# Statistics products behind the row transform, 2 KB pieces of mode weights, and whole 128-column products in a two-part convolution kernel

## The chip, the cores and the metric

The kernel runs on one core of one Trainium2 chip. The metric is the device time of one execution in microseconds (us). A core has TensorE (PE, matrix products into PSUM), VectorE (DVE), ScalarE (ACT), GpSimd (POOL) and SyncE (SP), which here issues the DMA transfers. The engines run their own instruction streams and wait for each other by semaphores.

## The reference

x is 8 images of 32 channels of 64x64, all float32. Group norm with 32 groups normalizes each channel of each image. Two residual parts follow each other:

```python
def _L0_conv_ref(x, weight, fc_w, fc_b):
    x_ft = jnp.fft.rfftn(x, axes=(-2, -1))
    blk = jnp.einsum('bimn,hiomn->bhomn', x_ft[:, :, :m1, :m2], w_c)
    ...
    xr = jnp.fft.irfftn(out_ft, s=(H, W), axes=(-2, -1))
    return jnp.einsum('bchw,oc->bohw', xr, fc_w) + fc_b[None, :, None, None]

def _L1_conv_ref(x, dft_weight, ksm_w, bias, fbm_scale):
    att = jax.nn.softmax(jax.nn.sigmoid(x.mean(axis=(2, 3)) @ ksm_w.T), axis=1)
    agg = jnp.einsum('bk,koihwc->boihwc', att, dft_weight)
    kernels = jnp.clip(jnp.fft.ifft2(cw, axes=(-2, -1), norm='ortho').real, -10.0, 10.0)
    ...
    return (out + bias[None, :, None, None]) * fbm_scale

x = x + _L0_conv_ref(_gn(x), L0_conv_weight, L0_conv_fc_w, L0_conv_fc_b)
x = x + _L1_conv_ref(_gn(x), L1_conv_dft_weight, L1_conv_ksm_w, L1_conv_bias, L1_conv_fbm_scale)
```

## The kernel before, in words

The order of work is written out by hand for each engine. The first part works on 32 by 32 modes of each channel; the second has one 3x3 convolution per image. A float32 product is two records of the trace, and each has a weight load (LDWEIGHTS, PEld) and a pass (MATMUL, PE). A product can use all 128 columns of the array, or 64 or 32 of them; products on different column parts run side by side. Each stage of the first part is a Fourier transform along one axis, written as products with constant matrices.

1. **Row transform**, `f1(k)` (L797, products on L807), eight pieces: 32 products of 64 columns by 64 each, all into PSUM slot 2, half a piece in each bank. ACT copies the first half out (`copy_y`, L420), DVE the second (L545). ACT squares x (L431), DVE sums the squares (L552).
2. **Statistics**, `sums(s)` (L811), after two pieces each: a product for the means (L817) and one for the squares (L819), both with a 128-column stationary matrix. DVE reads them in `pick(s)` (L557 to L562). After the fourth, variance, square root and reciprocal (L577, L578, L440, L580) give the factor 1/std that every operand needs.
3. **Column transform**, `f2` (L822 to L849): for each k of 0 to 3 and xx of 0, 1 a PSUM bank, filled for 8 images by two 64-column products each, 32 products per k. `pair(k, s)` makes two images of both banks of k.
4. **Operands**, `operand(n)` with n = 2k + xx (L583): DVE writes the normalized bank to `zn` (L591), which has two buffers, and the block of group 0 (32 partitions) straight to `bd[k]` (L594). ACT copies groups 1 to 3 from `zn` to `bd[k]` (L449). The two buffers make DVE wait for ACT's `bd_act`. POOL clears x_buf, the home of bd[2] and bd[3] (L357, L359), after operand 0.
5. **Modes**, `mix(ml)` (L851): 64 products of 32 columns with the mode weights in w_buf. It waits for operands 2ml and 2ml+1, for its weights, and for its slot: mix(3) takes slot 0, which DVE must first have emptied of mix(0) (`mixed_dve` 2, L621). DVE's copies out of the mix stand behind all operands and behind three small steps on constants (L610, L614, L615). ACT makes the copy (3,0) on L456.
6. `fc` (L867), waiting for all mix copies and for `fcd_ready` (L610), then the inverse transforms `i1` and `i2`, and then the attention kernels and the convolution `conv` (L953), with the rest of the time. The diff doesn't touch them.

SP issues, in this order: the rows of x, the four mode weights of 1 MB (L305), late constants, the kernel weights `dft_w` (1152 KB, L308), params; and then, after `mix_done` 6 and 8, x once more (L318).

The functions that the diff touches:

Of the kernel before, what the change touches and what calls it, by code (L numbers as in the profile page):

```python
# [102 lines left out]
def spectral_then_attention_conv(nc, x, w_modes, dft_w, params, consts, out):  # L103
    with ExitStack() as ctx:
# [34 lines left out]
        def const(name):  # L139
# [17 lines left out]
              for t in (bd_buf[:], r_buf[:], x_buf[:, 0:4096], x_buf[:, 4096:8192])]  # L157
        zn = [t_buf[:, at:at + 512].rearrange("p (n b r) -> p n b r", n=M1, b=B) for at in (2304, 2816)]
        ost = bd_buf[:, 0:2048].rearrange("p (s n) -> p s n", s=2)

        def x_part(k):
# [103 lines left out]
        def mixed_part(ml, xx):  # L265

            ps = slot[slot_of["mix", ml]][:, 512 * xx:512 * xx + 512]
            return mixed[:, :, :, 4 * xx + ml, :], ps.rearrange("p (nl b g) -> p nl b g", nl=8, b=B)
# [28 lines left out]
        def _(sp):  # L297
# [6 lines left out]
            for ml in range(4):  # L304
                sp.dma_start(modes[:, ml].rearrange("p n xo -> p (n xo)"), w_modes[:, ml]).then_inc(modes_in[ml], 16)  # L305
                if ml == 1:
                    sp.dma_start(cst[:, LATE:NCONST], consts[:, LATE:NCONST]).then_inc(cst_in, 16)
# [109 lines left out]
        def _(act):  # L417
# [23 lines left out]
            def blocks(n):  # L441

                k, xx = divmod(n, 2)
                act.wait_ge(zn_ready, n + 1)
                if k >= 2:
                    act.wait_ge(bd_zero, k + 1)
                for g in range(1, 4):
                    ps = slice(32 * g, 32 * g + 32)
                    ins = act.activation(bd[k][ps, g, xx], zn[n % 2][ps], ACT.Copy)  # L449
                ins.then_inc(bd_act, 1)  # L450
# [82 lines left out]
        def _(v):  # L533
# [9 lines left out]
            def copy_y(k):  # L543
                v.wait_ge(f1_done, 2 * k + 2)
                nc.vector.tensor_copy(*y_part(k, 1)).then_inc(y_dve, 1)  # L545
# [19 lines left out]
            for k in range(7):  # L565
                sum_squares(k)
                copy_y(k)
                if k == 2:
                    v.wait_ge(fwd_w_in, 16)
                if k in (3, 5, 6):  # L570
                    pick(k // 2 - 1 if k < 6 else 2)
            sum_squares(7, 0)
            sum_squares(7, 1)
            copy_y(7)
            pick(3)

# [6 lines left out]
            def operand(n):  # L583

                k, xx = divmod(n, 2)
                z = f2_bank(k, xx).rearrange("p (b r n) -> p n b r", r=2, b=B)
                rstd = rstd1.unsqueeze(1).unsqueeze(3).broadcast_to([128, M1, B, 2])
                v.wait_ge(f2_done, n + 1)
                if n >= 2:
                    v.wait_ge(bd_act, n - 1)  # L590
                nc.vector.tensor_tensor(zn[n % 2], z, rstd, ALU.mult).then_inc(zn_ready, 1)  # L591
                if k >= 2:
                    v.wait_ge(bd_zero, k + 1)
                ins = nc.vector.tensor_tensor(bd[k][0:32, 0, xx], z[0:32], rstd[0:32], ALU.mult)  # L594
                if n == 0:
                    chain(ins)
                    chain(nc.vector.scalar_tensor_tensor(out=dc1, in0=mean1, scalar=float(NPIX), in1=rstd1,
                                                         op0=ALU.mult, op1=ALU.mult))

                    dc = bd[0][0:32, 0, 0, 0, :, 0]  # L600
                    ins = nc.vector.tensor_tensor(dc, dc, dc1[0:32], ALU.subtract)  # L601
                ins.then_inc(bd_ready, 1)

            v.wait_ge(bd_zero, 2)
            for n in range(8):
                operand(n)

            v.wait_ge(cst_in, 16)
            v.wait_ge(prm_in, 16)
# [6 lines left out]

            for ml in range(4):
                for xx in range(2):
                    if (ml, xx) != (3, 0):
                        v.wait_ge(mix_done, 2 * ml + xx + 1)  # L620
                        nc.vector.tensor_copy(*mixed_part(ml, xx)).then_inc(mixed_dve, 1)  # L621
            for k in range(4):
# [173 lines left out]
        def _(pe):  # L796
# [25 lines left out]
            def f2_part(k, xx, s):  # L822

                ps = f2_bank(k, xx)
                ml = 4 * xx + k
                for b in (2 * s, 2 * s + 1):
                    col = 64 * b
                    for h in range(2):
                        f = 4 * ml + 2 * h
                        last = pe.matmul(ps[64 * h:64 * h + 64, col:col + 64],  # L830
                                         y_rows[:, b, f:f + 2, :].rearrange("w g c -> w (g c)"), const("fwd_w")[:, 0:64],
                                         start=True, stop=True)
                if s == 3:
                    last.then_inc(f2_done, 1)
# [133 lines left out]
            f1(5)  # L968
            f1(6)
            sums(2)  # L970
            pair(0, 2)
            f1(7)
            for s in range(3):
                pair(1, s)
            sums(3)
            pair(0, 3)
            pair(1, 3)
            f2(2)
            f2(3)
            for ml in range(4):  # L980
                mix(ml)
# [78 lines left out]
```

## Time and profile before

| | us |
|---|---|
| median of 3 runs | 147.77 |
| lowest, highest | 147.33, 148.44 |
| the profiled execution, whole | 147.89 |
| its span in the trace | 146.1 |

| engine | busy us | share of the span |
|---|---|---|
| PE | 125.8 | 86% |
| PEld | 91.6 | 63% |
| DVE | 78.3 | 54% |
| ACT | 68.2 | 47% |
| POOL | 44.5 | 30% |

The shares are means over stages with different limits, so each stage has to be read by itself: the chain of work that ended last says what released each step, the timeline of an engine says when its groups began, how long they took together and what ended the idle time before them, and a table of windows gives the granted TensorE clock (PEclk) of a stretch, 1.00 for 2.4 GHz and 0.50 for 1.2 GHz. "issue" is time in which an engine waited for nothing that the profile shows. Of the DMA queues, q1 carries the kernel's transfers and q8 carries blocks of instructions.

### The profile page before, as it was taken

To read this page: it belongs to the slowest core of one execution; us is meant where nothing else is said; L and a number is where in the kernel's file an instruction comes from. 1 tells how busy PE (TensorE), PEld (TensorE's weight loads), DVE (VectorE), ACT (ScalarE), POOL (GpSimd) and SP (SyncE) were. 2 spreads that over 40 slices of the span, in tenths; PEclk is the share of its full clock that TensorE was granted. 3 is DMA by queue.
4 is the path that set the end of the run, shared out by engine and by line. 5 is a ranking of instruction groups with operands and counts; after the bars stand their busy time and mean duration, and the time that the engine had idled before them with its cause. 6 is when DMAs were issued, how large, how long until landed. Compare 5 with 4: busy or idle time off the path is not lost.

```text
span 146.1 us, 4992 instructions
## 1 busy us (share of the span) xinstructions
PE 125.8 (86%) x2172; PEld 91.6 (63%) x2172; DVE 78.3 (54%) x194; ACT 68.2 (47%) x134; POOL 44.5 (30%) x40
## 2 busy tenths in 40 slices
PE   0899999594996479899999979997999999999970
PEld 0889998594986369799999968932234322333310
DVE  0089679358758944633378468995751842201220
ACT  0575754519999415513347751499720560111010
POOL 7980000007999999999300000000000000000000
PEclk9999999999599869999999999999999999999999
DMA  4999989996000388868705977295898106563384
GB/s 97 273 265 238 242 216 408 416 416 246 5 0 9 78 179 186 194 152 191 174 12 114 173 141 155 62 176 80 174 170 185 24 18 145 129 144 71 89 177 99
DMA packets 68837, 23.09 MB, mean 158 GB/s; under 512 B 67408, under 2 KB 67664, under 8 KB 68304
## 3 DMA queue, kind: packets, MB, share of 16 engines
q1 hardware_dynamic: 68816, 22.78, 64.7%
q8 instruction: 17, 0.28, 0.8%
q14 instruction: 4, 0.03, 0.1%
HBM read 14.38 MB, written 4.19 MB: 127 GB/s over the span
## 4 chain that ended last, share of the span: by engine, by line
PE 62%; ACT 13%; DVE 12%; issue 7%; DMA 2%; SPq 1%; ACTq 0%; DVEq 0%
PE slot L953 21%; PE slot L807 10%; PE slot L883 10%; PE slot L896 7%; PE slot L872 4%; ACT bd_buf L449 3%; PE slot L830 2%; DMA x_buf<-x 2%; PE slot L863 2%; ACT r_buf L449 2%; ACT conv_w L499 2%; ACT q_buf L476 2%; ACT x_buf L449 2%; DVE y_buf L641 2%; DVE conv_w L728 2%
## 5 line engine op out<-in xcount | busy, mean ns | idle before, releaser
L953 PE MATMUL slot<-w_buf,conv_w 128*32 128x512 f32 x192 | 42.3, 593 | 0.0
L953 PE MATMUL slot<-y_buf,conv_w 128*32 128x512 f32 x192 | 42.2, 593 | 0.0
L953 PEld LDWEIGHTS slot<-w_buf,conv_w 128*32 128x32 f32 x192 | 12.1, 109 | 22.1 <-issue 21.9
L807 PE MATMUL slot<-cst,x_buf 128*64 128x64 f32 x512 | 18.8, 238 | 4.8 <-DMA x_buf<-x 4.2
L807 PEld LDWEIGHTS slot<-cst,x_buf 128*64 128x64 f32 x512 | 18.1, 152 | 5.0 <-issue 5.0
L752 DVE TENSOR_SCALAR bd_buf<-slot,st 128x512 f32<-128x512 f32 x8 | 6.0, 748 | 19.9 <-PE slot L953 19.9
L896 PE MATMUL slot<-cst,t_buf 128*128 128x128 f32 x128 | 15.5, 278 | 0.8 <-issue 0.8
L896 PEld LDWEIGHTS slot<-cst,t_buf 128*128 128x128 f32 x128 | 14.7, 192 | 1.4 <-issue 1.2
L883 PE MATMUL slot<-cst,r_buf 128*64 128x128 f32 x256 | 14.6, 274 | 0.7 <-ACT r_buf L461 0.7
L883 PEld LDWEIGHTS slot<-cst,r_buf 128*64 128x64 f32 x256 | 13.9, 137 | 1.0 <-ACT r_buf L461 0.9
L552 DVE TENSOR_REDUCE row_sq<-q_buf 128x16 f32<-128x1024 f32 (+1 forms) x9 | 9.8, 1098 | 7.8 <-ACT q_buf L431 7.7
L476 ACT ACTIVATE q_buf<-y_buf 128x512 f32<-128x512 f32 x16 | 9.9, 622 | 7.8 <-DVE y_buf L641 7.8
L508 ACT ACTIVATE bd_buf<-slot,st 128x512 f32<-128x512 f32 x8 | 5.3, 681 | 17.5 <-PE slot L953 12.4
L641 DVE SCALAR_TENSOR_TENSOR y_buf<-slot,stat,x_buf 128x512 f32<-128x512 f32 x16 | 11.2, 747 | 2.4 <-PE slot L896 2.4
L953 PEld LDWEIGHTS slot<-y_buf,conv_w 128*32 128x32 f32 x192 | 10.6, 109 | 2.6 <-issue 2.6
L499 ACT ACTIVATE conv_w<-kern 32x96 f32<-32x96 f32 x24 | 6.7, 280 | 9.8 <-DVE kern L723 9.2
L357 POOL MEMSET x_buf<- 128x4096 f32 x1 | 3.5, 3517 | 23.2 <-DVE bd_buf L601 23.2
L631 DVE COPY t_buf<-slot 128x512 f32<-128x512 f32 x8 | 5.5, 692 | 8.2 <-PE slot L883 8.2
L863 PE MATMUL slot<-x_buf,w_buf 128*32 128x64 f32 x256 | 5.7, 258 | 3.6 <-DVE q_buf L621 2.1
L467 ACT ACTIVATE t_buf<-slot 128x512 f32<-128x512 f32 x8 | 4.8, 595 | 8.2 <-PE slot L883 8.2
L431 ACT ACTIVATE q_buf<-x_buf 128x1024 f32<-128x1024 f32 (+1 forms) x9 | 8.5, 954 | 0.0
L830 PE MATMUL slot<-cst,y_buf 128*64 128x64 f32 x192 | 7.0, 224 | 1.5 <-issue 1.5
(115 smaller groups left out, 188.5 us busy)
## 6 DMA issues: line engine op xcount, KB each, us to landing
x_buf<-x SPq DMA_DIRECT2D x16, 256.0 KB, 4.1
w_buf<-w_modes SPq DMA_DIRECT2D x4, 1024.0 KB, 9.8
x_buf<-x SPq DMA_DIRECT2D x32, 128.0 KB, 3.3
w_buf<-y_buf SPq DMA_DIRECT2D x16, 256.0 KB, 5.6
out<-bd_buf SPq DMA_DIRECT2D x28, 128.0 KB, 2.8
t_buf<-dft_w SPq DMA_DIRECT2D x1, 1152.0 KB, 14.2
out<-bd_buf SPq DMA_DIRECT2D x8, 64.0 KB, 1.9
cst<-consts SPq DMA_DIRECT2D x1, 388.0 KB, 9.0
```

The lines of the kernel that those rows point to most:

```text
L431: act.activation(sq, src, ACT.Square).then_inc(sq_ready, 1)
L449: ins = act.activation(bd[k][ps, g, xx], zn[n % 2][ps], ACT.Copy)
L476: act.activation(sq_trash[:, 512 * y:512 * y + 512].rearrange("p (u w) -> p u w", u=8), xa[:, 4 * g + 2 * y + x, 8 * half:8 * half + 8, 1: ...
L499: act.activation(conv_w[1][32 * j:32 * j + 32, 96 * (4 * g + i):96 * (4 * g + i) + 96], kt[32 * i:32 * i + 32, 96 * kh:96 * kh + 96], ACT. ...
L552: nc.vector.tensor_reduce(dst, sq, AX_X, ALU.add).then_inc(sq_used, 1)
L641: nc.vector.scalar_tensor_tensor(out=xa[:, b, us, 1:W + 1], in0=ps[:, :, y, :], scalar=mean1[:, b:b + 1], in1=xr[:, b, us, :], op0=ALU.sub ...
L807: last = pe.matmul(ps[64 * ri:64 * ri + 64, col:col + 64], x_part(k)[:, i, q, :], const("fwd_h")[:, 64 * ri:64 * ri + 64], start=True, sto ...
L830: last = pe.matmul(ps[64 * h:64 * h + 64, col:col + 64], y_rows[:, b, f:f + 2, :].rearrange("w g c -> w (g c)"), const("fwd_w")[:, 0:64], ...
L863: last = pe.matmul(ps[32 * nq:32 * nq + 32, col:col + 64], modes[:, ml, n, 32 * xx:32 * xx + 32], bd[ml][:, :, xx, n].rearrange("p g b r - ...
L883: last = pe.matmul(ps[64 * ri:64 * ri + 64, 128 * i:128 * i + 128], r_modes[:, g, c0 + i].rearrange("p y n -> p (y n)"), const(matrix), st ...
L896: last = pe.matmul(ps[:, 128 * u:128 * u + 128], t_rows[:, g, x, h:h + 4, :].rearrange("p j c -> p (j c)"), const("inv_w"), start=True, st ...
L953: last = pe.matmul(ps[32 * j:32 * j + 32, 512 * half:512 * half + 512], cw[r][:, b, kw, :], src[:, b, u:u + 8, kw:kw + W], start=(kw == 0) ...
```

## The change

The order of `sums` and `f1` on PE, the form of `f2` for k of 1 to 3, the place of `mix(0)`, eight `zn` buffers in place of two, a second block by DVE for odd operands, the place of DVE's mix copies, and the layout and pieces of the mode weights:

```diff
-        zn = [... for at in (2304, 2816)]
+        zn = [... t_buf[:, 4096 + 512 * n:4608 + 512 * n] ... for n in range(8)]
+        def own_blocks(n):
+            return (0, 1) if n % 2 else (0,)
...
-                sp.dma_start(modes[:, ml].rearrange("p n xo -> p (n xo)"), w_modes[:, ml]).then_inc(modes_in[ml], 16)
+                sp.dma_start(modes[:, ml].rearrange("p (q n) xo -> p q (n xo)", q=4), w_modes[ml].rearrange("q p n -> p q n")
+                             ).then_inc(modes_in[ml], 16)
...
-                for g in range(1, 4):
+                for g in range(len(own_blocks(n)), 4):
                     ps = slice(32 * g, 32 * g + 32)
-                    ins = act.activation(bd[k][ps, g, xx], zn[n % 2][ps], ACT.Copy)
+                    ins = act.activation(bd[k][ps, g, xx], zn[n][ps], ACT.Copy)
...
-                if k in (3, 5, 6):
-                    pick(k // 2 - 1 if k < 6 else 2)
+                if k in (3, 5):
+                    pick(k // 2 - 1)
             sum_squares(7, 0)
             sum_squares(7, 1)
             copy_y(7)
+            pick(2)
             pick(3)
...
-                if n >= 2:
-                    v.wait_ge(bd_act, n - 1)
-                nc.vector.tensor_tensor(zn[n % 2], z, rstd, ALU.mult).then_inc(zn_ready, 1)
+                nc.vector.tensor_tensor(zn[n], z, rstd, ALU.mult).then_inc(zn_ready, 1)
                 if k >= 2:
                     v.wait_ge(bd_zero, k + 1)
-                ins = nc.vector.tensor_tensor(bd[k][0:32, 0, xx], z[0:32], rstd[0:32], ALU.mult)
+                for g in own_blocks(n):
+                    ps = slice(32 * g, 32 * g + 32)
+                    ins = nc.vector.tensor_tensor(bd[k][ps, g, xx], z[ps], rstd[ps], ALU.mult)
...
+            def copy_mixed(ml, xx):
+                v.wait_ge(mix_done, 2 * ml + xx + 1)
+                nc.vector.tensor_copy(*mixed_part(ml, xx)).then_inc(mixed_dve, 1)
+            for ml in range(3):
+                copy_mixed(ml, 0)
+                copy_mixed(ml, 1)
             v.wait_ge(cst_in, 16)
...
-            for ml in range(4):
-                for xx in range(2):
-                    if (ml, xx) != (3, 0):
-                        v.wait_ge(mix_done, 2 * ml + xx + 1)
-                        nc.vector.tensor_copy(*mixed_part(ml, xx)).then_inc(mixed_dve, 1)
+            copy_mixed(3, 1)
...
                 for b in (2 * s, 2 * s + 1):
-                    col = 64 * b
+                    col, f = 64 * b, 4 * ml
+                    if k:
+                        last = pe.matmul(ps[:, col:col + 64], y_rows[:, b, f:f + 4, :].rearrange("w g c -> w (g c)"),
+                                         const("fwd_w")[:, 0:64], start=True, stop=True)
+                        continue
...
             f1(5)
             f1(6)
+            f1(7)
             sums(2)
-            pair(0, 2)
-            f1(7)
-            for s in range(3):
-                pair(1, s)
             sums(3)
-            pair(0, 3)
-            pair(1, 3)
+            for k in range(2):
+                for s in range(2 - 2 * k, 4):
+                    pair(k, s)
             f2(2)
+            mix(0)
             f2(3)
-            for ml in range(4):
+            for ml in range(1, 4):
                 mix(ml)
...
-    modes = array("L0_conv_weight")[0].reshape(C, C, 4, 2, 4, M1).transpose(2, 0, 4, 5, 3, 1).reshape(128, 4, 2048)
+    modes = array("L0_conv_weight")[0].reshape(C, C, 4, 2, 4, M1).transpose(2, 0, 4, 5, 3, 1)
+    modes = modes.reshape(128, 4, 4, 512).transpose(1, 2, 0, 3)
```

The same bytes of mode weights travel, now as pieces of 2 KB instead of 8 KB. The products of f2 for k of 1 to 3 become 48 of 128 columns instead of 96 of 64, so with their loads 192 instructions instead of 384; PE's stream goes from 2172 product records to 2076.

On PE, from the second half of f1(6) to the first product of mix(3), the order before was this (a row is a run of like products with their tiles; slot2 is f1's and f2(2)'s, slot0 and slot1 those of f2(0) and f2(1)):

```order
L807 MATMUL slot2<-cst,x_buf 64x64 x15
L817 MATMUL aggp<-y_buf,ones_re 128x64 [waits stat_read,y_dve,y_act]
L819 MATMUL aggp<-row_sq,ones_par 128x32 [waits sq_used]
L830 MATMUL slot0<-cst,y_buf 64x64 x8
L807 MATMUL slot2<-cst,x_buf 64x64 [waits y_act,xh_in14]
...
L830 MATMUL slot1<-cst,y_buf 64x64 x24
L817 MATMUL small<-y_buf,ones_re 128x64 [waits stat_read,y_dve,y_act]
L819 MATMUL small<-row_sq,ones_par 128x32 [waits sq_used]
...
L863 MATMUL slot0<-bd_buf,w_buf 32x64 [waits bd_act,modes_in0,bd_ready]
```

and in the change, the same stretch is this:

```order
L816 MATMUL slot2<-cst,x_buf 64x64 [waits y_dve,xh_in15]
L816 MATMUL slot2<-cst,x_buf 64x64 x15
L826 MATMUL aggp<-y_buf,ones_re 128x64 [waits stat_read,y_dve,y_act]
L828 MATMUL aggp<-row_sq,ones_par 128x32 [waits sq_used]
L826 MATMUL small<-y_buf,ones_re 128x64 [waits stat_read,y_dve,y_act]
L828 MATMUL small<-row_sq,ones_par 128x32 [waits sq_used]
L842 MATMUL slot0<-cst,y_buf 64x64 x16
L838 MATMUL slot1<-cst,y_buf 128x64 x16
L838 MATMUL slot2<-cst,y_buf 128x64 [waits y_dve,y_act]
L838 MATMUL slot2<-cst,y_buf 128x64 x15
L875 MATMUL slot0<-bd_buf,w_buf 32x64 [waits bd_act,modes_in0,bd_ready]
L838 MATMUL aggp<-cst,y_buf 128x64 [waits stat_read]
```

The last statistics stand directly behind f1(7) and ahead of what is left of f2(0) and all of f2(1), and mix(0) stands ahead of f2(3).

On DVE, behind the last operand, the order before was this:

```order
L594 TENSOR_TENSOR x_buf<-small,stat1 32x512 [waits bd_zero]
L610 TENSOR_TENSOR fc_diag<-prm,cst 128x128 [waits prm_in,cst_in]
L614 TENSOR_TENSOR bconst<-prm 128x1
L615 TENSOR_TENSOR bconst<-bconst,prm 128x1 [waits dve_done]
L621 COPY q_buf<-slot0 128x64x8 [waits mix_done,dve_done]
L621 COPY q_buf<-slot0 128x64x8 [waits mix_done]
```

and in the change it is this:

```order
L600 TENSOR_TENSOR x_buf<-small,stat1 32x512 [waits bd_zero]
L600 TENSOR_TENSOR x_buf<-small,stat1 32x512
L616 COPY q_buf<-slot0 128x64x8 [waits mix_done] x2
L616 COPY q_buf<-slot1 128x64x8 [waits mix_done] x2
L616 COPY q_buf<-slot2 128x64x8 [waits mix_done] x2
L623 TENSOR_TENSOR fc_diag<-prm,cst 128x128 [waits prm_in,cst_in]
L627 TENSOR_TENSOR bconst<-prm 128x1
L628 TENSOR_TENSOR bconst<-bconst,prm 128x1 [waits dve_done]
L616 COPY q_buf<-slot0 128x64x8 [waits mix_done,dve_done]
```

Six of the seven mix copies now stand ahead of the three steps on constants.

## Rows read from the trace of the kernel before

**Rows 1.** The page: busy time of PE, and the DMA queues
```profile
PE 125.8 (86%) x2172; PEld 91.6 (63%) x2172; DVE 78.3 (54%) x194; ACT 68.2 (47%) x134; POOL 44.5 (30%) x40
q8 instruction: 17, 0.28, 0.8%
```

**Rows 2.** Chain of work that ended last, 26 to 64 us: start, us, what
```profile
26.54 0.81 PE slot L830 x26
27.35 1.48 issue
28.83 0.91 PE slot L830 x22
29.75 0.36 PE small L817 x2
...
31.96 0.70 DVE t_buf L591
...
48.40 1.30 DVE q_buf L621 x2
...
49.75 3.38 PE slot L863 x125
53.15 0.70 DVE q_buf L621
54.06 6.50 PE slot L872 x56
```

**Rows 3.** Timeline of PE: start, us together, form, records, idle before
```profile
22.81 0.69 PE L807 MATMUL slot<-cst,x_buf 128*64 128x64 f32 x17 [0.17 <-issue]
24.50 2.04 PE L807 MATMUL slot<-cst,x_buf 128*64 128x64 f32 x64
30.24 3.02 PE L830 MATMUL slot<-cst,y_buf 128*64 128x64 f32 x96
35.41 0.97 PE L830 MATMUL aggp<-cst,y_buf 128*64 128x64 f32 x26 [1.99 <-issue]
37.74 3.38 PE L863 MATMUL slot<-bd_buf,w_buf 128*32 128x64 f32 x128
45.28 2.33 PE L863 MATMUL slot<-x_buf,w_buf 128*32 128x64 f32 x128 [1.50 <-ACT x_buf L449]
```

**Rows 4.** Timeline of PEld, weight loads of 128 columns, two records each
```profile
12.81 0.30 PEld L817 LDWEIGHTS aggp<-y_buf,ones_re 128*128 128x128 f32 x2
13.02 0.30 PEld L819 LDWEIGHTS aggp<-row_sq,ones_par 128*128 128x128 f32 x2
```

**Rows 5.** Timeline of DVE and ACT
```profile
24.78 1.28 DVE L552 TENSOR_REDUCE row_sq<-q_buf 128x8 f32<-128x512 f32 x2
26.59 0.69 DVE L545 COPY y_buf<-slot 128x512 f32<-128x512 f32 x1 [0.53 <-PE slot L807]
34.16 0.67 DVE L594 TENSOR_TENSOR bd_buf<-slot,stat 32x512 f32<-32x512 f32 x1
46.35 0.87 DVE L610 TENSOR_TENSOR fc_diag<-prm,cst 128x128 f32<-128x128 f32 x1
41.08 7.99 ACT L449 ACTIVATE x_buf<-t_buf 32x512 f32<-32x512 f32 x12
```

**Rows 6.** DMA queues, windows 9.9:22.8, 26.4:27.4, 33.0:34.1 and 38:49: packets, MB, share
```profile
q8 instruction: 3, 0.05, 1.5%
q8 instruction: 1, 0.02, 5.5%
q8 instruction: 1, 0.02, 5.0%
q8 instruction: 3, 0.05, 1.8%
```

**Rows 7.** Table of windows: us, busy by engine, granted clock, DMA share, GB/s
```profile
36.70:40.10 3.40, 3.40 (x111) 3.28 (x111) 2.61 (x4) 3.34 (x5) 3.34 (x2) 0.50 0.00 0
50.30:53.80 3.50, 2.79 (x110) 2.54 (x100) 2.45 (x5) 0.61 (x1) 3.25 (x4) 0.51 0.85 192
```

More of the change, by code:

```diff
@@ L157, in spectral_then_attention_conv @@
               for t in (bd_buf[:], r_buf[:], x_buf[:, 0:4096], x_buf[:, 4096:8192])]
-        zn = [t_buf[:, at:at + 512].rearrange("p (n b r) -> p n b r", n=M1, b=B) for at in (2304, 2816)]
+        zn = [t_buf[:, 4096 + 512 * n:4608 + 512 * n].rearrange("p (n b r) -> p n b r", n=M1, b=B) for n in range(8)]
         ost = bd_buf[:, 0:2048].rearrange("p (s n) -> p s n", s=2)
+        def own_blocks(n):
+            return (0, 1) if n % 2 else (0,)
         def x_part(k):
@@ L826, in f2_part @@
                 for b in (2 * s, 2 * s + 1):
-                    col = 64 * b
+                    col, f = 64 * b, 4 * ml
[3 more added lines that the diff above has]
+                        continue
                     for h in range(2):
-                        f = 4 * ml + 2 * h
                         last = pe.matmul(ps[64 * h:64 * h + 64, col:col + 64],
-                                         y_rows[:, b, f:f + 2, :].rearrange("w g c -> w (g c)"), const("fwd_w")[:, 0:64],
-                                         start=True, stop=True)
+                                         y_rows[:, b, f + 2 * h:f + 2 * h + 2, :].rearrange("w g c -> w (g c)"),
+                                         const("fwd_w")[:, 0:64], start=True, stop=True)
                 if s == 3:
```

## The prediction, made before the change was run

> **What bounds the kernel now.** I read the page first: PE is busy for 86% of the span, but every edit lies before `fc` [rows 1]. So I read the chain of work that ended last from 26 to 64 us, and then the timelines of PE, DVE and ACT over the same stretch. The reader is to see that PE products are only a part of that chain. From 26.54 to 29.75 us it runs through two pieces of the column transform and a hole of 1.48 us named "issue", and only then through the last statistics, whose result every operand needs (first operand at 31.96). From there to 48.40 it runs through the operand copies of ACT, 12 of which take 7.99 us, or 0.666 each [rows 2, 5]. DVE then does its constant steps and its copies of mix(0), and only at 49.75 may mix(3) start. `fc` starts at 54.06. Behind `fc` no order, form or size changes, except that x is loaded again from the end of mix(2); so I take the time after 54.06 as it is and ask when `fc` starts. The profiled execution took 147.89 us with a span of 146.1, 0.12 above the median of 147.77, so a gain read from it is taken off the median.
>
> **The holes on PE.** There are two, 1.48 us before 28.83 and 1.99 us before 35.41 [rows 2, 3]. Queue q8 carries 17 packets of 0.28 MB together; PE has 2 times 2172 records, and 4344 by 17 is 256: one block of instructions per 256 loads and passes [rows 1]. Between the resumption at 22.81 and the hole stand 17 records of f1(6), 4 of sums, 16 of pair(0,2), 64 of f1(7) and 26 of pair(1, ·), 127 or one block. The block packet of the first hole lies in the window 26.4 to 27.4 and the one of the second in 33.0 to 34.1 [rows 6], and PE resumes about 1.4 us after each packet. So these holes are late instructions. Without big packets around them, blocks come faster: 3 in the 12.9 us of 9.9:22.8, 4.3 us each, under loads of x, and 3 in the 11 us of 38:49, about 3.8 us each [rows 6]. Around the holes it was 6.0 us (22.81 to 28.83) and 6.6 (28.83 to 35.41), while the 8 KB pieces of the modes and then dft_w moved.
>
> The Trainium skill (Runtime: NRT & Kernel Launch, Instruction fetch mechanics) says that instructions come in 16 KiB blocks of 256 and that the crossing is mostly hidden. The trace agrees on the block and not on the hiding. Were it hidden, the rival "blocks do not pace" below would be the forecast.
>
> **1. Statistics earlier.** Before, f1(7) began at 24.50, because sums(2) and pair(0,2) stood between. Now it begins behind f1(6) at 23.43 (22.81 plus 0.6 for the 17 records), takes 2.04 and ends at 25.5 [rows 3]. sums(2) follows, to 26.0. sums(3) needs DVE's copy of f1(7). DVE is free for it: without pick(2), the square sums of 24.78 start 0.63 earlier and end at 25.4; the copy starts 0.1 after f1(7) and takes 0.69, to 26.3 [rows 5]. So sums(3) starts at 26.3 instead of 29.75, and the first operand at 26.3 + (31.96 - 29.75) = 28.5. pick(2), 0.63 us on DVE, fits between the copy and the end of sums(3), 0.6 later. Its operand also needs f2(0): 32 records of 0.031 (26 in 0.81) [rows 2] behind sums(3), at 27.9. **Gain so far 3.45 us**, and the hole of 1.48 is part of it.
>
> **2. Column transform as whole products.** This is the edit that costs. The trace of before has no 128-column load with 64 columns passed, except the statistics: two pairs of loads start 12.81 and 13.02, so 0.105 to 0.11 per record [rows 4]. A half product moves at 0.031 per record, two at a time. Thus 64 records of halves, 1.95 us per k, become 32 of 0.11, 3.5 us per k. The lower bound is the pace of the halves with half as many records doing the double work, 0.059 per record or 1.9 us per k; I take 0.11, since the statistics are the same shape. For k = 1 to 3 that is 10.5 us on PE instead of 5.8.
>
> The skill (TensorE: Matmul & The Clock Gate, LDWEIGHTS) gives columns/1.2 ns for a load, 107 ns for 128. The row says 105 to 110; by the page f2 would cost 3.4 us per k.
>
> f2(1) runs 27.9 to 31.4, f2(2) to 34.9.
>
> **3. Operands.** Without the `bd_act` waits DVE does 2 steps for even n and 3 for odd, 0.65 each (two copies in 1.30) [rows 2], ACT 3 and 2 at 0.666. DVE ends operand 1 at 32.3, operand 3 at 35.5 and 5 at 38.8; ACT follows by 0.3 to 0.9. From here f2 sets the time. mix(0) runs 34.9 to 37.3 at the 2.33 of the undisturbed mix [rows 3]; f2(3) gives its banks at 39.1 and 40.8, so operand 7 ends at 43.0 and ACT's last block at 43.3, against 49.1 before. POOL's two clearings (3.5 to 4.1 each) start after operand 0 and end at 38, ahead of operand 6.
>
> **4. Mixes, now paced by their instructions.** mix(1) to mix(3) now stand back to back: 128 records in 2.33 us is 256 instructions, and a block comes each 3.8 us. I count blocks of 128 records: one ends after 39 records of mix(1), the next ones after 39 of mix(2) and of mix(3). Asking for the next when it enters one, about 32 records ahead of the array, PE asks at 40.9 and gets it at 44.7 (wanted at 43.9), the next at 48.5 (wanted at 47.0). mix(1) runs 40.8 to 43.2, mix(2) to 46.3, mix(3) to **50.1**. DVE's copies of mix(0) end at 44.3, before mix(3) wants its slot. The other copies are followed by the constant steps, now behind mix(2): 47.2 plus 2.1 (from 46.35 to 48.40) is 49.3 [rows 2, 5], hidden by mix(3), and the bound if mix(3) came earlier. The last copy and its wait take 0.91 (53.15 to 54.06) [rows 2]: **`fc` at 51.0 instead of 54.06, a gain of 3.05 us**.
>
> **5. What costs nothing.** The 2 KB pieces carry the same bytes, and SP's issues of the modes run under a DMA queue that is full anyway; the weights of mix(0) are wanted at 34.9. If more, smaller packets cost 10% on the 13 us of modes and dft_w, mix(3) still has its weights, and only POOL's start would be touched, which waits for mix(0). The first reload of x starts with the end of mix(2), 46.3 against 47.7; it is wanted 20 us later.
>
> The sum: 147.8 - 3.05 = **144.7 us**.
>
> **The rivals.**
> - *Blocks do not pace in a quiet DMA.* For: mix(2) ran all of its 128 records in 2.33 us. Against: blocks came no faster than one in 3.6 us, even where PE was not waiting for anything else. Then mix(3) ends at 47.9, DVE's constants (48.5) and the last copy set `fc` to 49.4: 143.1 us.
> - *Whole products go at the pace of halves*, 1.9 us per k. f2(2) ends at 31.9, DVE becomes the bound with its 20 steps (operand 7 at 41), the constants end at 46.6, blocks allow mix(3) to end at 46.1 and `fc` starts at 47.5: 141.3 us. Against it stand both loads in the statistics [rows 4].
> - *A stretch at the half clock in mix(3) or fc.* Before, the clock fell to 0.50 and 0.51 behind idle of 1.99 and 2.1 us and stayed there for 3.4 [rows 7]. The holes of 0.8 and 1.5 that I expect, with the 0.9 before `fc`, lie close together. fc at half pace for most of 2.8 us costs 1.4: 146.1 us.
> - *The smaller pieces don't help the blocks.* The block for pair(1, ·) then comes at 28.8 as before, 0.9 later than PE wants it. Steps 2 to 4 shift by that: 145.6 us.
> - *Slower: f2 itself holds the clock low.* A whole product passes 64 columns in the time in which it loads 128, so the array passes columns about half of the time, and its clock may fall without any hole. At half clock the load of 128 columns doubles; each us so spent costs 0.5. The gain of 3.05 is gone with 6 us at half clock of the 20 from 28 to 48; with all of it (f2 7 us per k, mixes 3.38) `fc` starts near 63: up to 157 us. Nothing in the trace speaks for it: the falls there have a hole each.
>
> **Numbers.** Forecast 0.54, with a range of its own of 143.6 to 145.9; blocks do not pace 0.12; whole products fast 0.10; half clock at mix(3) or fc 0.12; pieces don't help 0.07; slower 0.05. The range takes in the upper cases and the fast one's edge: 141.6 to 146.8. A change of under 1% (1.5 us) can hardly be told from none here. Faster by over 1% means under 146.3: all of the first, second, third and fifth and half of the fourth, less something for terms I haven't seen: 0.83. Same 0.12, slower 0.05.
>
> **What would show it.** Right: the hole before 28.83 gone, the product for the last statistics near 26.3 and the first operand near 28.5; whole products at 0.11 per record, so f2(1) at 3.5 us; no wait of DVE for `bd_act`; holes named "issue" in mix(2) and mix(3), none before; `fc` near 51. Wrong: whole products at 0.06 per record; PEclk below 1.00 between 28 and 47; mixes back to back without a hole; or a hole before pair(1, ·) still there.

## The result and the profile after

| | before | changed |
|---|---|---|
| median of 21 runs, us | 147.4 | 146.37 |
| lowest, highest | 146.58, 149.65 | 145.12, 152.8 |
| profiled execution, whole | 147.89 | 149.09 |
| its span | 146.1 | 147.3 |

The ratio to the kernel before is 0.9905, with a 95% interval of 0.9879 to 0.9932: 1.4 us less, where 3.05 were forecast. Such a ratio leaves out, on both sides, the executions over 1.5% above the fastest of the same kernel, while the medians take in all of them and lie 1.0 us apart. The gain is clear of the scatter, but it is under the 1% (a time under 146.3 us) that the prediction set as its line between faster and same, and it had given "same" 0.12.

The profiled execution of the changed kernel, at 149.09 us, was one of the long ones, so the same kernel was profiled once more, in an execution of 145.44 us. Both are read here, because they begin to differ at one place only.

The timeline of PE of the first (start, us together, line and form, records, idle before and what ended it):

```profile
19.05 3.61 PE L816 MATMUL slot<-cst,x_buf 128*64 128x64 f32 x110
25.68 3.74 PE L816 MATMUL slot<-cst,x_buf 128*64 128x64 f32 x81 [3.02 <-issue]
...
30.25 0.41 PE L826 MATMUL small<-y_buf,ones_re 128*128 128x64 f32 x2 [0.28 <-issue]
...
31.87 7.36 PE L838 MATMUL slot<-cst,y_buf 128*128 128x64 f32 x64
...
55.24 7.38 PE L884 MATMUL slot<-fc_diag,q_buf 128*128 128x128 f32 x64 [1.03 <-DVE q_buf L616]
```

And of the second, where L816 is `f1`, L826 the means of `sums`, L838 the whole products of `f2`, L875 `mix` and L884 `fc`:

```profile
22.62 2.73 PE L816 MATMUL slot<-cst,x_buf 128*64 128x64 f32 x81 [0.17 <-issue]
...
26.18 0.41 PE L826 MATMUL small<-y_buf,ones_re 128*128 128x64 f32 x2 [0.27 <-issue]
...
27.79 7.60 PE L838 MATMUL slot<-cst,y_buf 128*128 128x64 f32 x64
35.32 2.27 PE L875 MATMUL slot<-bd_buf,w_buf 128*32 128x64 f32 x128
37.53 2.00 PE L838 MATMUL aggp<-cst,y_buf 128*128 128x64 f32 x16
39.36 1.95 PE L838 MATMUL small<-cst,y_buf 128*128 128x64 f32 x16
41.24 2.30 PE L875 MATMUL slot<-r_buf,w_buf 128*32 128x64 f32 x127
...
44.99 2.20 PE L875 MATMUL slot<-x_buf,w_buf 128*32 128x64 f32 x127 [0.89 <-issue]
48.70 1.84 PE L875 MATMUL slot<-x_buf,w_buf 128*32 128x64 f32 x95 [1.51 <-issue]
51.59 7.38 PE L884 MATMUL slot<-fc_diag,q_buf 128*128 128x128 f32 x64 [1.04 <-DVE q_buf L616]
```

The second is the sum almost row by row. The hole of 1.48 us ahead of the last statistics [rows 2] is gone, those statistics start at 26.18, whole products take 0.115 us each (the 7.36 of the first profile by 64; the 7.60 of the second hold a hole of 0.14, shown below), there are two holes in the mixes, and `fc` starts at 51.59 instead of 54.06. The first has the same stages, all later, behind a hole of 3.02 us in f1(6), where before had 0.17 [rows 3]. From the start of `fc` to the end it takes 92.0 us in the second (143.6 - 51.59), 92.1 in the first and 92.0 before, so the whole matter is when `fc` starts.

On DVE and ACT in the second profile, the first operand, the last one, the six copies ahead of the constants, and ACT's last blocks:

```profile
28.50 0.69 DVE L595 TENSOR_TENSOR t_buf<-slot,stat 128x512 f32<-128x512 f32 x1
...
42.01 1.36 DVE L600 TENSOR_TENSOR x_buf<-small,stat 32x512 f32<-32x512 f32 x2
43.40 3.09 DVE L616 COPY q_buf<-slot 128x512 f32<-128x512 f32 x5
46.75 0.69 DVE L616 COPY q_buf<-slot 128x512 f32<-128x512 f32 x1 [0.26 <-PE slot L875]
...
40.29 3.37 ACT L454 ACTIVATE x_buf<-t_buf 32x512 f32<-32x512 f32 x5 [0.84 <-DVE t_buf L595]
```

ACT ends its blocks at 43.7, where 12 blocks for x_buf alone ran to 49.07 before [rows 5]. In the chain of work that ended last, from 22 us to `fc`, no piece of ACT is left and none of DVE but the last copy: it runs over PE's products and the holes.

### The profile page after: what moved, and what is told of

It reads as the page before. It is cut to its first block, busy times and chain, and to the rows that moved or that the text cites. A ratio compares the mean times of both kernels' runs of the same rounds, so it can differ in the third digit from the quotient of the medians.

```text
span 147.3 us, 4794 instructions
## 1 busy us (share of the span) xinstructions
PE 128.7 (87%) x2076; PEld 94.6 (64%) x2076; DVE 79.6 (54%) x198; ACT 65.0 (44%) x130; POOL 44.0 (30%) x40
## 4 chain that ended last, share of the span: by engine, by line
PE 72%; DVE 9%; issue 7%; ACT 6%; DMA 2%; SPq 1%; DVEq 0%; ACTq 0%
PE slot L965 21%; PE slot L895 10%; PE slot L816 10%; PE slot L908 7%; PE slot L875 6%; PE slot L838 5%; PE slot L884 4%; DMA x_buf<-x 2%; ACT conv_w L504 2%; ACT q_buf L481 2%; DVE y_buf L650 2%; PE slot L842 2%; DVE conv_w L737 2%; PE aggp L938 1%; PE aggp L838 1%
## 5 line engine op out<-in xcount | busy, mean ns | idle before, releaser
L965 PEld LDWEIGHTS slot<-w_buf,conv_w 128*32 128x32 f32 x192 | 12.0, 109 | 22.5 <-issue 22.3
L816 PE MATMUL slot<-cst,x_buf 128*64 128x64 f32 x512 | 19.6, 243 | 7.6 <-DMA x_buf<-x 4.2
L816 PEld LDWEIGHTS slot<-cst,x_buf 128*64 128x64 f32 x512 | 18.9, 157 | 8.1 <-issue 7.9
L425 ACT ACTIVATE y_buf<-slot 128x512 f32<-128x512 f32 x8 | 4.8, 595 | 10.3 <-PE slot L816 10.3
L550 DVE COPY y_buf<-slot 128x512 f32<-128x512 f32 x8 | 5.5, 689 | 6.9 <-PE slot L816 6.9
```

What stands on the lines that cost most here:

```text
L816: last = pe.matmul(ps[64 * ri:64 * ri + 64, col:col + 64], x_part(k)[:, i, q, :], const("fwd_h")[:, 64 * ri:64 * ri + 64], start=True, sto ...
L965: last = pe.matmul(ps[32 * j:32 * j + 32, 512 * half:512 * half + 512], cw[r][:, b, kw, :], src[:, b, u:u + 8, kw:kw + W], start=(kw == 0) ...
```

## The experiments

### The block of f1(6), and the kernel once more

The changed kernel without any edit, for a second profile.

> The changed kernel itself, once more, for a second profile. The profile on record has a hole of 3.02 us in f1(6), where the block of instructions came 4.6 us after it was wanted because the mode weights had begun to move 0.9 us before. Theory A (a block waits whenever it is asked for while the mode weights or dft_w move, whatever their pieces): holes of 1 to 3 us again between 22 and 32 us, their place depending on whether the request falls before or behind the first mode packet; if before, no hole in f1(6) and one of about 1.5 us near pair(1, .). Theory B (the hole in f1(6) is a disturbance of that one execution): no hole over 0.3 us before f2(1), first operand near 28.5, fc near 51.

It took 145.44 us; the rows are above. The hole in f1(6) is 0.17 us, as Theory A has it for a request that falls ahead of the modes. The second half of Theory A was wrong for this kernel: near pair(1, ·), where PE resumes 6.1 us after 22.62, the chain of work that ended last shows 0.14 us of idle and not 1.5, so that up to `fc` this one profile looks as Theory B has it too:

```profile
28.56 0.14 issue
28.70 6.69 PE slot L838 x59
```

The DMA queues show the same event in both executions, at different times. Packets by queue (queue, packets, MB, share of the 16 engines) of the first profile in the windows 18.7:23.2 and 23.2:24.4:

```profile
q1 hardware_dynamic: 1515, 1.16, 94.8%
...
q8 instruction: 1, 0.02, 5.0%
```

and of the second in 18.7:20.3 and 20.3:21.4:

```profile
q1 hardware_dynamic: 1198, 0.32, 97.6%
...
q8 instruction: 1, 0.02, 5.5%
```

No block of instructions moved in the first window of either; it moved behind 23.2 in one and behind 20.3 in the other, and in both PE resumed 2.3 to 2.4 us after its packet began. SP had issued the first mode weight at 18.00 in the first and at 18.22 in the second.

### The kernel before once more

> The kernel before, once more, for a second profile. If the hole before the last statistics belongs to every execution (as the sum took it), 1.4 to 1.6 us of issue stand again near 27 us and fc starts near 54. If its length is drawn anew in each execution, by when the block is asked for and how much is queued ahead of it, the hole is shorter or longer by 0.5 us or more here, and fc starts earlier or later by the same; the gain read from one profile then overstates or understates that of the medians.

It took 148.59 us, and `fc` starts at 54.72:

```profile
24.75 0.69 PE L807 MATMUL slot<-cst,x_buf 128*64 128x64 f32 x17 [2.09 <-issue]
...
30.77 0.91 PE L830 MATMUL slot<-cst,y_buf 128*64 128x64 f32 x22 [1.48 <-issue]
...
51.35 2.38 PE L863 MATMUL slot<-x_buf,w_buf 128*32 128x64 f32 x128 [2.17 <-DVE q_buf L621]
54.72 5.48 PE L872 MATMUL slot<-fc_diag,q_buf 128*128 128x128 f32 x47 [0.99 <-DVE q_buf L621]
```

Two things. The kernel before has the hole in f1(6) too, in some executions: 2.09 us here. And mix(3) took 2.38 us here, at full clock, against 3.38 in the profile that the sum was made from, whose clock had fallen to 0.51 [rows 2, 7]. The hole of 1.48 was there in both. So the base of the sum held 1 us that not every execution has. The mean granted clock of the first profile, with two stretches at half clock, was 0.976, and that of the second 0.999; of 23 further executions of the kernel before, 6 lie at 0.975 or below and 8 at 0.995 or above.

Taken over all profiles with ungated issue, the hole in f1(6) goes with the time at which SP issues the first mode weight (SP's row in the timeline). Of these, a5 and the i kernels are experiments told below:

| profile | first mode weight issued, us | hole in f1(6), us |
|---|---|---|
| a5, chained | 17.59 | 1.82 |
| changed, first | 18.00 | 3.02 |
| before, second | 18.02 | 2.09 |
| a3, halves | 18.10 | 1.10 |
| i4, constants late | 18.21 | none |
| changed, second | 18.22 | 0.17 |
| before, first | 18.64 | 0.17 |
| i1, interleaved | 18.70 | 0.28 |
| i3, interleaved and chained | 18.76 | 0.55 |
| u1, old order | 18.77 | 0.28 |
| a2, 8 KB | 19.16 | 0.17 |

At 18.10 and before it is 1.1 to 3.0 us, at 18.21 and behind it at most 0.55. SP runs the same instructions up to that issue in all of them, so the half microsecond is not a matter of the edits. Eleven profiles show that the two go together; whether the one makes the other is what the gated runs below ask, and the table can't tell.

### Pieces of 8 KB

```diff
-sp.dma_start(modes[:, ml].rearrange("p (q n) xo -> p q (n xo)", q=4), w_modes[ml].rearrange("q p n -> p q n"))
+sp.dma_start(modes[:, ml].rearrange("p n xo -> p (n xo)"), w_modes[:, ml])
...
```

The layout of the weights in memory goes back with it.

> The changed kernel with the mode weights in 8 KB pieces again, all else kept. Theory A: blocks wait about as long with either piece, so the time is within 0.5% of the changed kernel, near 146.4 us. Theory C (smaller pieces shorten the wait, by letting the block in sooner): slower than the changed kernel by 1 to 2 us, and longer holes.

Median 146.01 us, ratio to before 0.9909 (0.9868 to 0.9951): the same as the changed kernel's 0.9905. (One of the 12 executions took 453.49 us, which nothing here explains.) With the block asked for near 22.5, it moved behind 26.7 here and behind 26.4 with 2 KB pieces and with the kernel before's 8 KB [rows 6]. The windows 22.8:26.4 and 26.4:27.5 of the changed kernel, second profile:

```profile
q1 hardware_dynamic: 692, 1.39, 103.6%
...
q8 instruction: 1, 0.02, 5.4%
```

692 packets went ahead of the block where the kernel before has 245 larger ones, 1.4 MB in both, and it waited as long. Theory C falls: the size of the pieces is worth nothing that shows. The only thing in the profile that might be its doing is a hole of 0.69 us in f2(1) here, and a kernel with 2 KB pieces (i1 below) has one of 0.69 too.

### Half products

```diff
-                    if k:
+                    if k > 9:
                         last = pe.matmul(ps[:, col:col + 64], ...)
```

> The changed kernel with f2(1) to f2(3) as 64-column products again, 192 instructions more. By the terms of the sum, f2 takes 5.8 instead of 10.5 us on PE, but three quarters of a block more have to come at 3.8 to 6 us a block. Theory 1 (blocks pace this stretch, so whole products pay for themselves): within 1 us of the changed kernel, with new issue holes in f2 and the mixes that add up to 3 to 4 us. Theory 2 (the slow loads of whole products are what ate the gain): faster than the changed kernel by 2 to 4 us.

Median 146.95 us, ratio 0.9977 (0.9927 to 1.0027), so 0.6 us above the changed kernel by the medians. The intervals barely overlap, and Theory 2, with 2 to 4 us less, is out. Theory 1 holds, with longer holes than it said. Its profile (an execution of 150.87 us, with 1.10 in f1(6)) has these holes up to mix(3):

```profile
30.67 3.83 PE L842 MATMUL slot<-cst,y_buf 128*64 128x64 f32 x123 [1.22 <-issue]
...
36.67 2.08 PE L875 MATMUL slot<-bd_buf,w_buf 128*32 128x64 f32 x124 [1.91 <-issue]
...
40.40 1.03 PE L842 MATMUL aggp<-cst,y_buf 128*64 128x64 f32 x28 [1.38 <-issue]
...
47.96 2.19 PE L875 MATMUL slot<-x_buf,w_buf 128*32 128x64 f32 x127 [1.71 <-issue]
51.97 1.24 PE L875 MATMUL slot<-x_buf,w_buf 128*32 128x64 f32 x63 [1.82 <-issue]
```

Their sum is 8.0 us, against 2.5 in the second profile of the changed kernel, from f2 to mix(3). The records of f2(1) to f2(3) take some 6.1 us of PE here, where the 96 of whole products take 11.1; all of these 5 us and a little more go into waiting for instructions. This execution was long for another reason too: from 53.3 to 60.0 the granted clock was 0.50, so that 94.9 us passed from the start of `fc` (54.24) to the end of the span, and not 92.0.

### Issue of the big transfers behind f1(6)

```diff
+            sp.wait_ge(f1_done, 14)
             for ml in range(4):
                 sp.dma_start(modes...
```

> The changed kernel, with the four mode weights, the late constants, dft_w and the parameters issued only after f1(6) is done (f1_done 14), about 24 us. The DMA queue then has nothing in it while PE fetches the block that f1(6) needs. Theory A (waiting behind these transfers makes the holes): no hole in f1(6), first operand near 28.5 to 29, weights of mix(0) still there in time at 35, faster than the changed kernel by 1 to 2.5 us, 144 to 145 us; a hole may be left behind 28 us, where the transfers now run. Theory B: no change, since there was nothing to repair in most executions.

Median 146.19 us, 12 runs from 145.18 to 146.85, ratio 0.9955 (0.9917 to 0.9994). The median did not move, so the 1 to 2.5 us of Theory A didn't come, and for the median Theory B was right. The spread did move: 1.7 us between the lowest and the highest, where the changed kernel had 7.7 in 21 runs and 5 of them at 149 and above. That fits Theory A in this: the long executions are those in which the block of f1(6) is behind the modes. It is not shown for each, since only one long execution was profiled. The profile here, of the longest of the 12 at 146.85, has 0.55 us in f1(6), and the two holes of the mixes, 1.53 and 1.39.

The same line in the kernel before:

> The kernel before, with the mode weights, late constants, dft_w and the parameters issued after f1(6) (f1_done 14), as was done to the changed kernel. This takes the race for the block of f1(6) out of both, so that the pair gives the worth of the rest of the change. If the race is what scatters the executions, they lie within 2 us of each other here too, none above 149. Pair difference by the sum without the half clock in mix(3): 2 us (gated before near 148.2, since the changed one gave 146.2). If the statistics order with its hole was worth nothing, the difference is under 0.7 us.

Median 146.42 us, ratio 0.9924 (0.9879 to 0.9969), 145.04 to 148.88. This is the miss that tells most. I expected 148.2. One line on SP gives the kernel before about as much as the whole change gave (0.9924 and 0.9905, with intervals that overlap widely): gated, the two kernels are at 146.42 and 146.19. The spread of 3.8 us is also wider than I said, and here it goes with the clock: the four executions from 147.72 to 148.88 have a mean granted clock of 0.971 to 0.984, and 9 of the 12 lie at 0.988 or below, while all 12 of the gated changed kernel lie at 0.992 or above. Its profile, an execution of 146.25 us:

```profile
26.62 1.57 PE L831 MATMUL slot<-cst,y_buf 128*64 128x64 f32 x48
...
33.44 0.97 PE L831 MATMUL aggp<-cst,y_buf 128*64 128x64 f32 x26 [1.57 <-issue]
...
39.65 1.09 PE L864 MATMUL slot<-bd_buf,w_buf 128*32 128x64 f32 x58 [2.89 <-issue]
...
43.34 1.16 PE L864 MATMUL slot<-r_buf,w_buf 128*32 128x64 f32 x60 [1.49 <-issue]
...
46.79 2.25 PE L864 MATMUL slot<-x_buf,w_buf 128*32 128x64 f32 x127 [1.19 <-issue]
50.27 1.20 PE L864 MATMUL slot<-x_buf,w_buf 128*32 128x64 f32 x63 [1.23 <-issue]
52.41 7.38 PE L873 MATMUL slot<-fc_diag,q_buf 128*128 128x128 f32 x64 [0.94 <-DVE q_buf L622]
```

All 48 records ahead of the last statistics run in one piece of 1.57 us: the hole of 1.48 is gone, its block having moved at 24.3, ahead of the first packets of the modes. The holes stand later now, 8.4 us of them. ACT's operand copies do not hide them: from 26 us to `fc` at 52.41 the chain of work that ended last runs on PE alone, through every one of these holes, and through one copy of DVE at the end. Two of its pieces:

```profile
36.76 2.89 issue
39.65 2.21 PE slot L864 x108
```

So in this profile the kernel before, too, is paced by its instructions over this stretch, and ACT's copies, which stood on the chain from 32.7 to 45 us in its first profile, are off it.

### One transfer at a time

```diff
+                if ml:
+                    sp.wait_ge(modes_in[ml - 1], 16)
...
+            sp.wait_ge(modes_in[3], 16)
             sp.dma_start(dft_sb...
```

> The changed kernel, with each mode weight, and dft_w, issued only when the one before has landed, so that never more than 1 MB (some 64 KB per DMA engine) is queued and there is a pause between them. Theory Q (a block waits behind what is queued ahead of it): each wait for a block is at most 2.6 us and the slow executions of the changed kernel (149 to 152 us) vanish, median 145 to 146. Theory R (a block gets its turn among the pieces, so that depth is without effect): waits of 3.6 to 4.6 us as before wherever a transfer moves, median as that of the changed kernel, 146.4.

Six runs, 144.83 to 148.61 us, median 147.64; the ratio that comes out, 0.9825 (0.9741 to 0.9909), rests on two of them, and I draw nothing from the times. The profile of 147.46 us speaks against Theory Q: a hole of 1.82 us in f1(6), with only one 1 MB block of mode weights issued by then.

### The order of the statistics

The changed kernel with `sums`, `f1(7)`, `pair` and `pick` in the old order.

> The changed kernel with the statistics, f1(7), pair and pick in the old order, all else kept (whole products, eight zn, two blocks by DVE, late constants). Theory S (the first operand sets the chain, as in step 1 of the sum): the first operand comes near 31.4 and fc 3 us later, slower than the changed kernel by 2 to 3 us. Theory P (from f1(6) on, the work on PE is what is full: the first part of f2, its slow loads and the mixes, and the order within it is free): PE has no wait behind sums(3), f2(2) starts at 31 to 31.5 as in the changed kernel, fc within 0.5 us and the time the same within 0.5%.

Median 145.74 us, ratio 0.9918 (0.9874 to 0.9963): no different from the changed kernel. Theory P holds, within a little: PE waits 0.66 us for ACT ahead of mix(0), and `fc` comes 0.64 us later than in the second profile, where it had said 0.5. From its profile (146.07 us), the PE rows and the first operand on DVE:

```profile
26.61 2.89 PE L837 MATMUL slot<-cst,y_buf 128*128 128x64 f32 x24
...
35.80 2.29 PE L874 MATMUL slot<-bd_buf,w_buf 128*32 128x64 f32 x128 [0.66 <-ACT bd_buf L454]
...
49.48 1.75 PE L874 MATMUL slot<-x_buf,w_buf 128*32 128x64 f32 x95 [1.66 <-issue]
52.23 7.38 PE L883 MATMUL slot<-fc_diag,q_buf 128*128 128x128 f32 x64 [1.01 <-DVE q_buf L615]
```

```profile
31.57 0.69 DVE L594 TENSOR_TENSOR t_buf<-slot,stat 128x512 f32<-128x512 f32 x1
```

The first operand comes 3.07 us later than in the second profile of the changed kernel, and `fc` only 0.64 later. The 24 slow records ahead of the statistics run without a hole, since their block had the time to arrive. What step 1 of the sum counted as 3.45 us is, in the changed kernel, worth 0.6 at most: PE has f2 and the mixes to do either way.

### Another order

```diff
-            f2(2)
-            mix(0)
-            f2(3)
-            for ml in range(1, 4):
-                mix(ml)
+            f2(2, (0,))
+            mix(0)
+            f2(2, (1,))
+            f2(3, (0,))
+            mix(1)
+            f2(3, (1,))
+            mix(2)
+            mix(3)
```

with DVE's copies of mix(0) ahead of operand 6 and of mix(1) and the constants ahead of operand 7.

> A new order in place of the changed kernel's: PE makes f2(2) bank 0, mix(0), f2(2) bank 1, f2(3) bank 0, mix(1), f2(3) bank 1, mix(2), mix(3); DVE copies mix(0) ahead of operand 6 and mix(1) and does its constants ahead of operand 7. The second profile of the changed kernel has holes of 0.89 and 1.51 us in mix(2) and mix(3), where two dense stages follow each other, and none in f2. If blocks come one per 3.8 us and only dense stretches starve, the first hole goes and the second shrinks to about 1 us, and fc starts at 49.8 to 50.2 instead of 51.6: 1.0 to 1.8 us faster than the changed kernel. If the holes are not a matter of density, the time stays within 0.5 us.

Median 146.64 us, ratio 0.9927 (0.988 to 0.9974): no gain. The profile (145.84 us) shows why:

```profile
40.78 2.23 PE L879 MATMUL slot<-r_buf,w_buf 128*32 128x64 f32 x128
42.94 2.00 PE L842 MATMUL small<-cst,y_buf 128*128 128x64 f32 x16
44.87 2.28 PE L879 MATMUL slot<-x_buf,w_buf 128*32 128x64 f32 x128
48.76 2.27 PE L879 MATMUL slot<-x_buf,w_buf 128*32 128x64 f32 x128 [1.61 <-ACT x_buf L454]
51.97 7.38 PE L888 MATMUL slot<-fc_diag,q_buf 128*128 128x128 f32 x64 [0.94 <-DVE q_buf L613]
```

The holes named issue are gone from the last three mixes, as the density theory said. In their place mix(3) waits 1.61 us for operand 7, which stood behind DVE's constants (44.90 to 46.48). With the constants behind operand 7:

> The interleaved order of the first try, but with DVE's constants behind operand 7 and the copies of mix(2), where the changed kernel has them. The first try had no holes in its mixes and lost it to operand 7, which started 1.6 us late behind the constants. Expected: operand 7 at 45.0 instead of 46.5, mix(3) at 47.3 instead of 48.8, fc near 50.7, 1 us faster than the changed kernel (144.5 in the fast executions). If a block is late in mix(3) once it is dense behind mix(2), fc stays at 51.5.

Six runs, median 145.36 us (144.78 to 146.2), ratio 0.9881 (0.9829 to 0.9934):

```profile
44.62 3.20 PE L879 MATMUL slot<-x_buf,w_buf 128*32 128x64 f32 x161
48.18 1.71 PE L879 MATMUL slot<-x_buf,w_buf 128*32 128x64 f32 x95 [0.37 <-issue]
50.92 7.38 PE L888 MATMUL slot<-fc_diag,q_buf 128*128 128x128 f32 x64 [1.03 <-DVE q_buf L613]
```

mix(2) and mix(3) have one hole of 0.37 between them, and `fc` starts at 50.92. The same with the gated issue:

> The same order with the gated issue. By the race theory no execution is above 147 us, and the median is that of the gated kernel less what the order brings: 145.2. If the later landing of the parameters (near 43.5 us) or of dft_w holds up the constants or POOL, it is no better than the gated kernel, 146.2.

Median 145.09 us (144.31 to 146.03, six runs), ratio 0.9858 (0.98 to 0.9916), with `fc` at 50.42 in the profile of 144.31 us. It has the lowest median of all. That it beats the changed kernel (0.9879 to 0.9932) is likely and not shown, since the intervals overlap. None of the 18 executions of the two gated forms of the changed kernel took over 147 us. The interleaved order with the chained issue was worse, for the reason that its expectation names:

> The interleaved order together with the chained issue. If both theories hold, the gains add: 143.5 to 145 us and no slow executions. If chaining delays dft_w past 42 us, POOL starts late and operand 7, which has the constants with their parameters ahead of it on DVE, waits for them: then no better than the interleaved order alone.

Median 151.08 us, ratio 1.0187 (1.012 to 1.0254). The parameters landed behind the chained dft_w, and DVE's constants waited for them with operand 7 queued behind (its profile is of an execution of 152.25 us):

```profile
50.04 0.61 DVE L627 TENSOR_TENSOR fc_diag<-prm,cst 128x128 f32<-128x128 f32 x1 [6.15 <-DMA prm<-params]
```

## Why the prediction was right in direction and too large in size

The median of 146.37 us lies inside the range of 141.6 to 146.8, near its upper end, and 1.7 us above the forecast of 144.7. Against the second profile, term by term:

| step | forecast | measured |
|---|---|---|
| 1: last statistics | 26.3 | 26.18 |
| 1: first operand | 28.5 | 28.50 |
| 2: whole product | 0.11 per record | 0.115 (7.39 by 64, the hole of 0.14 taken out) |
| 3: mix(0) starts | 34.9 | 35.32 |
| 3: operand 7 ends | 43.0 | 43.4 |
| 4: holes in mix(2), mix(3) | 0.8, 1.5 | 0.89, 1.51 |
| 4: fc starts | 51.0 | 51.59 |

- **The path through the changed kernel was right.** The chain left ACT and DVE as forecast. `fc` came 0.6 us later than the sum: about 0.5 because the 96 records of whole products take 0.005 us more each, the rest in small pieces.
- **The base was mis-sized.** The sum subtracted from an `fc` start of 54.06, and with it from a mix(3) of 3.38 us at half clock. With the same stage at full clock (2.38, second profile of before) the path through mix(3) is 1.0 us shorter, and with it the gain. I had the row with the clock of 0.51 and used it only for a rival in the changed kernel. It belonged in the sum's base: 3.05 less 1.0 is 2.05, and less the 0.6 by which `fc` came late, 1.45. That is about what undisturbed executions of the two kernels differ by: the lowest of 21 are 146.58 and 145.12, 1.46 apart, and the ratio gives 1.4. How often the base has this half clock in mix(3) was not measured, so the 1.0 is its worth in one execution and not in the median.
- **The hole in f1(6) was not in the sum.** Step 1 took the start of f1(7) from the 0.17 us of idle before 22.81. This is a draw: in some executions, of both kernels, it is 1.1 to 3.0 us. In the changed kernel it goes through whole to `fc` (3.65 us later in the first profile than in the second: 2.85 of it are the longer hole, and 1.0 the clock that fell behind it, since 81 records took 3.74 instead of 2.73 us; f2 and the mixes gave a little back). In the kernel before, the second profile's hole of 2.09 made `fc` only 0.66 later, since that execution was spared the half clock. It can reach the medians, which are 1.0 us apart, by way of the long executions; how much of that is its doing was not measured.
- **"The smaller pieces don't help the blocks" is what happened.** I gave it 0.07. The sum put no wait between 22.81 and f2(1) at 27.9, and so needed a block among 2 KB pieces in 5.1 us; it took 6.1 (22.62 to 28.70), as with 8 KB (6.0, 22.81 to 28.83 before). It cost next to nothing, 0.14 us, and not the 0.9 of the rival, since PE had five records of whole products before the border of the block and ran out only at 28.56. That this was so cheap was luck and not foreseen: the profiles a2 and i1, with the same five records ahead of the border, lose 0.69 us there.
- **Step 1 was the right time and the wrong worth.** The operands did start 3.45 us earlier than in the first profile of before, but the run with the old order shows that inside the changed kernel the order alone is worth 0.6 us at most, and by the medians nothing: behind it the work on PE decides, and that is the same with either order.
- **Which edit carries the gain is open.** Order of the statistics, pieces and whole products were each taken back alone, and none is worth more than 0.6 us. The eight `zn` with the split of the copies, the late constants and the place of mix(0) were not taken back. The profiles show ACT and DVE gone from the chain, which fits them, but the gated kernel before comes as low without any of these edits.
- **Blocks that do not pace, fast whole products, low clock in f2, half clock in mix(3) or `fc`**: none happened in the two profiles of the changed kernel. Granted clock from 28 to 52 us was 1.00 in the second profile. With its hole of 3.02 us the first had a granted clock of 0.64 from 25.7 to 29.3 us, in f1, which no term or rival had, and the kernel with half products had half clock in `fc`.

The Trainium skill (Runtime: NRT & Kernel Launch, Instruction fetch mechanics) calls the crossing of a block mostly hidden. Between 26 and 52 us that does not hold here, with 8.0 us of such holes in the profile with half products and 2.5 in the better one of the changed kernel.

## What to carry to other kernels

Count instructions as well as their time: where PE uses up 256 loads and passes in under 3.45 to 3.7 us, the time that a block took here in a quiet queue, it waits for its instructions. Slower products in smaller number can then cost nothing, and dense and sparse stages can be interleaved. Try one wait on the issuing engine that keeps big transfers out of the queues while a dense stage fetches its next block: it gave the kernel before 1.1 us and took the long executions out of the changed one, though not off its median. And profile the base twice: a microsecond of half clock or a late block in one profile is not the kernel's.

## What the runs showed of the hardware that I had not expected

- The wait of an instruction block does not depend on whether 2 KB or 8 KB pieces are moving: from the resumption between 22.5 and 22.9 to the packet it is 3.6 us (before) and 4.3 (a2) with 8 KB, 3.8 (changed, second) and 4.2 (i1) with 2 KB.
- A shift of the issue of a transfer by about 0.1 us (18.10 against 18.21) goes with a hole on another engine that is 1 us or more, or none.
- A late block paces PE again and again: in the gated kernel before, PE ran dry and resumed at 39.65, 43.34, 46.79 and 50.27, one block of 256 per 3.45 to 3.7 us, with queue q1 at 4.8% of its share or less from 40.8 to 47.7. The packets moved at 40.7, 44.3 and 47.9, about 1.0 us after a resumption, and PE resumed 2.4 to 2.7 us after each. Among big transfers the first part grew to 3.6 to 4.3 us, the second stayed at 2.2 to 2.4 (26.4 to 28.83 before, 26.45 to 28.70 in the changed kernel). The 3.8 of the prediction was slightly too slow, and its "no faster than one in 3.6" too: two packets of before moved at 33.1 and 36.5.
